# Sixteen-head attention with ALiBi: bias factors on GpSimd, replication in six DMAs

## The reference, cut to what matters

```python
# B = 16, S = 256, C = 128, H = 16 heads of D = 8
x = x + single_head_attention(layernorm(x))       # block 1
x = x + routed_experts(layernorm(x))              # block 2, 8 experts, top 2
h = layernorm(x)                                  # the third norm
qkv = h @ in_proj_weight.T + in_proj_bias
rel = pos[:, None] - pos[None, :]
bias = minimum(rel * slopes[h], 8.0)              # slopes[h] = 2 ** (-0.5 * (h + 1))
scores = q @ k.T * D ** -0.5 + bias
x = x + softmax(scores) @ v @ out_proj_weight.T + out_proj_bias   # block 3
x = x + one_of_8_experts(layernorm(x))            # block 4
```

## Time and profile before

| | us |
|---|---|
| median of 3 runs | 988.57 (988.5 to 989.13) |
| profiled execution, its own time | 988.53 |
| its span, first to last instruction | 986.5 |
| block 3, first to last `score` (L1569) | 477.3 to 784.4 |
| PE busy | 783.2 (79%) |
| DVE busy | 549.3 (56%) |
| ACT busy | 395.9 (40%) |
| POOL busy | 357.9 (36%) |
| DMA queue of SP, share of 16 engines | 27.3% |

### The profile page before, as it was taken

How to read it: one execution, slowest core, us unless ns; L and a number is a source line. 1 busy time by engine, 2 the same in 40 slices (tenths; PEclk the granted TensorE clock), 3 DMA queues, 4 the chain that set the end, 5 groups by cost and what they waited for, 6 DMA issues and landing times.

```text
span 986.5 us, 19021 instructions
## 1 busy us (share of the span) xinstructions
PE 783.2 (79%) x5641; PEld 564.8 (57%) x5641; DVE 549.3 (56%) x2190; ACT 395.9 (40%) x947; POOL 357.9 (36%) x543
## 2 busy tenths in 40 slices
PE   0798479999999999952489999999999982038894
PEld 0676355555666677742246676667666651028883
DVE  4688573233322332333588989898987714026672
ACT  0456121222212322210036666766676661025562
POOL 5000517777850134433222423242322102744552
PEclk9999668999999999986569999999999995559997
DMA  9970001111100132303654444444443014111110
GB/s 250 155 221 0 0 1 36 40 41 41 44 0 14 52 112 78 96 30 90 128 106 95 90 108 93 102 83 106 95 85 67 3 45 155 54 53 55 50 50 14
DMA packets 75114, 72.44 MB, mean 73 GB/s; under 512 B 8125, under 2 KB 65680, under 8 KB 72732
## 3 DMA queue, kind: packets, MB, share of 16 engines
q1 hardware_dynamic: 69436, 60.38, 27.3%
q0 software_dynamic: 5600, 11.12, 3.5%
HBM read 43.71 MB, written 27.33 MB: 72 GB/s over the span
## 4 chain that ended last, share of the span: by engine, by line
PE 52%; DVE 18%; issue 12%; DMA 5%; POOL 5%; ACT 3%; DVEq 2%; SPq 2%; POOLq 0%; ACTq 0%
PE bank L1475 10%; PE bank L1476 9%; DVE rt L1065 6%; PE bank L1498 6%; PE bank L1527 4%; PE bank L1617 3%; PE bank L1569 3%; POOL sorted_rows L766 3%; PE bank L1604 3%; PE bank L1599 2%; DMA arena<-arena 2%; SPq L548 1%; DVEq L1180 1%; PE bank L1435 1%; PE bank L1707 1%
## 5 line engine op out<-in xcount | busy, mean ns | idle before, releaser
L1065 DVE CUSTOM_DVE_ANT_0 rt<-bank,alibi 128x256 f32<-128x256 f32 x512 | 192.9, 419 | 44.4 <-PE bank L1569 37.5
L973 DVE TENSOR_TENSOR arena<-arena,bank 128x512 f32<-128x512 f32 (+1 forms) x128 | 75.0, 587 | 187.8 <-ACT arena L1253 187.8
L1280 ACT ACTIVATE arena<-bank 128x512 f32<-128x512 f32 x256 | 150.6, 598 | 55.4 <-PE bank L1604 49.5
L1253 ACT ACTIVATE arena<-bank 128x512 f32<-128x512 f32 (+1 forms) x128 | 66.1, 517 | 202.9 <-PE bank L1476 202.9
L1569 PE MATMUL bank<-arena 72*128 72x256 bf16 x512 | 104.7, 289 | 26.6 <-DMA arena<-qk_parts 13.4
L1599 PE MATMUL bank<-arena 81*128 81x256 bf16 x512 | 117.0, 274 | 8.3 <-ACT arena L1280 4.7
L1475 PE MATMUL bank<-arena 128*128 128x320 f32 (+2 forms) x256 | 115.7, 534 | 7.5 <-DVE arena L973 7.5
L1476 PE MATMUL bank<-arena 128*128 128x320 f32 (+2 forms) x256 | 111.9, 519 | 0.0
L1604 PE MATMUL bank<-arena,ident_b 128*128 128x256 bf16 (+8 forms) x544 | 80.2, 243 | 0.0
L1569 PEld LDWEIGHTS bank<-arena 72*128 72x128 bf16 x512 | 39.0, 102 | 69.4 <-DVE arena L1065 42.8
L1475 PEld LDWEIGHTS bank<-arena 128*128 128x128 f32 x256 | 42.8, 193 | 53.5 <-DVE arena L973 41.1
(11 more groups left out here) (242 smaller groups left out, 1402.9 us busy)
## 6 DMA issues: line engine op xcount, KB each, us to landing
arena<-qk_parts SPq DMA_DIRECT2D x48, 192.0 KB
arena<-qk_parts SPq DMA_DIRECT2D x144, 64.0 KB
qk_parts<-arena SPq DMA_DIRECT2D x16, 384.0 KB, 2.8
back_rows<-empty_row SPq DMA_DIRECT2D x1, 4096.0 KB, 37.8
arena<-back_rows SPq DMA_DIRECT2D x16, 256.0 KB, 3.8
arena<-in_w SPq DMA_DIRECT2D x2, 2048.0 KB, 10.9
xg_rows<-empty_row SPq DMA_DIRECT2D x1, 2580.0 KB, 38.5
arena<-xg_rows SPq DMA_DIRECT2D x8, 322.5 KB, 4.0
```

The lines of the kernel that those rows point to most:

```text
L973: nc.vector.tensor_tensor(out, sil[:, k, 0:out.shape[1]], bank[4 + k][:, 0:out.shape[1]], ALU.mult).then_inc(hid_done, 1)
L1065: last = nc.vector.tensor_tensor_reduce(biased[n % 2 * QT + u], bank[n % 2][:, SEQ * u:SEQ * u + SEQ], alibi[:, h, P * (1 - u):P * (1 - u) ...
L1253: nc.scalar.activation(sil[:, k, 0:width], bank[2 + k][:, 0:width], ACT.Silu).then_inc(sil_done, 1)
L1280: nc.scalar.activation(prT3[:, n % (2 * HG)].rearrange("p k t -> p (k t)"), bank[2 + n % 2][:], ACT.Exp).then_inc(exp3_done, 1)
```

## The change

The change touches block 3 and its constants.

- **Bias as a factor.** `FULL` goes from 4 to 2. Heads 2 to 8 get no strips on PE. A table `factor` = exp(min(8 - slope * rel, 0)) is built in advance on POOL and ACT, and `apply_factor` (POOL, L782) multiplies the capped columns of the probabilities of heads 2 to 8, after `exponent`, in place. `weigh` waits for `factored`. `prT3` has 12 buffers, not 8.
- **Slots.** `weigh` is cut in halves (`WEIGH_0`, `WEIGH_1`), three slots later than before; `project` in `project_v` and `project_qk`, one slot apart; `copy_qk` in `copy_q` and `copy_k`; `norm5` in two. Most other offsets move by a few slots. POOL goes by the slot table too, where it went batch by batch.
- **Third norm.** `normalise` runs on ACT; `root` on POOL makes scale and shift in four instructions, not one. `values` moves to ACT without its bias; `bv` goes through `w_out` once, ahead of block 3, and is added to `bo`. `v3` has five buffers.
- **Maxima.** `send_max` is issued by ACT, on its own queue, a slot after the copy.
- **Replication.** One DMA of 72 rows for `ks`, with a source that repeats three times; five for `qs`, of 16, 16, 16, 16 and 8 rows, three of them with a source that repeats twice.

```diff
@@
-FULL = 4
+FULL = 2
+PR = 3 * HG
+VRING = 5
...
-COMBINE_0, COMBINE_1, STATS, VARIANCE, NORM, TURN, HT, QKV, QK_COPY, VALUES = -41, -40, -39, -38, -33, -30, -29, -26, -25, -19
...
+COMBINE_0, COMBINE_1, STATS, VARIANCE, ROOT, NORM_0, NORM_1, OUTPUT_BIAS = -42, -41, -38, -37, -36, -34, -33, -29
+TURN, HT, VALUE, QK, Q_COPY, K_COPY, PARTS_QK, VALUES = -32, -31, -27, -26, -25, -24, -23, -21
...
@@
         def replicate(c):
...
             rows = part_dram[c % 2].rearrange("w a (d h) t -> w (a d) h t", d=HD)
-            for a in range(PARTS):
-                r = PARTS * HD * a
-                sp.dma_start(ks[r:r + PARTS * HD, c % RING], rows[1]).then_inc(qk3_in[c % RING], 16)
-                for k in range(PARTS):
-                    sp.dma_start(qs[r + HD * k:r + HD * k + HD, c % RING], rows[0, HD * a:HD * a + HD]).then_inc(qk3_in[c % RING], 16)
+            sp.dma_start(ks[0:KROWS, c % RING], rows[1].unsqueeze(0).to_broadcast([PARTS, PARTS * HD, NH, SEQ])).then_inc(qk3_in[c % RING], 16)
+            for b in range(0, PARTS * PARTS, 2):
+                first, last = b // PARTS, min(b + 1, PARTS * PARTS - 1) // PARTS
+                n = min(2, PARTS * PARTS - b)
+                src = rows[0, HD * first:HD * first + HD * n] if last > first else rows[0, HD * first:HD * first + HD].unsqueeze(0).to_broadcast([n, HD, NH, SEQ])
+                sp.dma_start(qs[HD * b:HD * (b + n), c % RING], src).then_inc(qk3_in[c % RING], 16)
...
@@
+        def apply_factor(n):
+            c, h = divmod(n, NH)
+            pool.wait_ge(exp3_done, n + 1)
+            if n == FULL:
+                pool.wait_ge(factor_set, 1)
+            for k in range(QT):
+                first = capped_from(h, k)
+                if first < SEQ:
+                    pr = prT3[:, n % PR, k, first:SEQ]
+                    last = nc.gpsimd.tensor_tensor(pr, pr, factor[:, h - FULL, first - P * k:SEQ - P * k], ALU.mult)
+            last.then_inc(factored, 1)
...
@@
-        def norm3(c):
...
-                last = nc.vector.tensor_scalar(h3[:, c % 2, u, :], x[:, 2 * c + u, :], mv[:, c % 2, u, 0:1], rstd3[:, c % 2, u:u + 1],
-                                               ALU.subtract, ALU.mult)
...
+        def normalise(c, u):
...
+            last = nc.scalar.activation(h3[:, c % 2, u, :], x[:, QT * c + u, :], ACT.Identity, scale=norm3[:, c % 2, u, 1:2],
+                                        bias=norm3[:, c % 2, u, 0:1])
...
+        def send_max(c):
+            wait_apart(act, (max_rows_done, c + 1))
+            act.dma_start(qs[MROW:KALL, c % RING], max_rows[0:PARTS * NH, c % 2]).then_inc(max_in[c % 2], 16)
...
@@
-                first = bias_from(h, k) if h < CLAMPED else SEQ
-                biases = range(BIAS_PARTS[h]) if first < SEQ else ()
+                biases = range(BIAS_PARTS[h]) if h < FULL else ()
...
+        def weigh(g, u):
...
+            if u == 0:
+                pe.wait_ge(exp3_done, HG * (g + 1))
+                if k * HG < CLAMPED:
+                    pe.wait_ge(factored, factors_to(HG * g + HG - 1))
```

More of the change, by code:

```diff
@@ L82, with capped_from, factors_to @@
 SLOPE_PARTS = [bf16_parts(s) for s in SLOPES]
[L83 to L89, removed]
+BIAS_PARTS = [len([v for v in SLOPE_PARTS[h] if v]) for h in range(FULL)]
+STRIP = [sum(BIAS_PARTS[:h]) for h in range(FULL)]
+FACTORS = CLAMPED - FULL
+def capped_from(h, k):
+    return min((P * k + int(MAX_BIAS / SLOPES[h]) + 1) // 2 * 2, SEQ)
+def factors_to(n):
+    c, h = divmod(n, NH)
+    return FACTORS * c + min(max(h + 1 - FULL, 0), FACTORS)
 def batch_at(slot, offset):
@@ L259, in _build @@
     bn3 = carve([P, 2, QT, 6])
-    mv = carve([P, 2, QT, 3])
-    rstd3 = carve([P, 2, QT])
+    mv = carve([P, 2, QT, 2])
+    norm3 = carve([P, 2, QT, 2])
     h3 = carve([P, 2, QT, D])
@@ L742, in root5 @@
         def root5(e):
-            shift, scale = xw[:, QT * e:QT * e + QT, D + 2], xw[:, QT * e:QT * e + QT, D + 3]
             pool.wait_ge(var5_done, e + 1)
[L747 to L756, removed]
+            root(mv5[:, e % 2], xw[:, QT * e:QT * e + QT, D + 2], xw[:, QT * e:QT * e + QT, D + 3], rstd5_done)
+        def apply_factor(n):
+            c, h = divmod(n, NH)
+            pool.wait_ge(exp3_done, n + 1)
[7 more added lines that the diff above has]
+            last.then_inc(factored, 1)
+        for slot3 in range(FIRST_SLOT, LAST_SLOT):
+            n = head_at(slot3, FACTOR)
+            if n is not None and FULL <= n % NH < CLAMPED:
+                apply_factor(n)
+            if (c := batch_at(slot3, PARTS_QK)) is not None:
                 parts(c)
-            if alive(c + 1, BATCH):
-                root(c + 1)
-            if alive(c, BATCH):
+            if (c := batch_at(slot3, ROOT)) is not None:
+                root3(c)
+            if (c := batch_at(slot3, OUTPUT_BIAS)) is not None:
                 output_bias(c)
-            if alive(c - ROOT_LAG, BATCH):
-                root5(c - ROOT_LAG)
+            if (c := batch_at(slot3, ROOT_5)) is not None:
+                root5(c)
         def send_sorted(i):
@@ L1129, in _ @@
                 norm3_variance(c)
-            if (c := batch_at(slot3, NORM)) is not None:
-                norm3(c)
-            if (c := batch_at(slot3, VALUES)) is not None:
-                values(c)
             if (c := batch_at(slot3, DIVIDE_0)) is not None:
@@ L1292, in turned, with values, copy_q @@
             if c >= 1:
-                act.wait_ge(v3_mm, c)
+                act.wait_ge(qk3_mm, c)
             nc.scalar.activation(hT3, bank[6][:, 0:SEQ], ACT.Copy).then_inc(hT3_done, 1)
-        def copy_qk(c):
+        def values(c):
+            act.wait_ge(v3_mm, c + 1)
+            if c >= VRING:
+                act.wait_ge(pv3_mm, NH // HG * (c - VRING + 1))
+            for u in range(QT):
+                last = nc.scalar.activation(v3[:, c % VRING, u, :, 0:HD],
+                                            bank[6][:, SEQ + D * u:SEQ + D * u + D].rearrange("p (h d) -> p h d", d=HD), ACT.Copy)
+            last.then_inc(v3_done, 1)
+        def copy_q(c):
             act.wait_ge(qk3_mm, c + 1)
```

224 lines of the change are left out of this document (123 added, 101 removed).

## The result

| | before | after |
|---|---|---|
| median, us | 988.57 | 1075.61 (1073.9 to 1088.77, 5 runs) |
| ratio, 95% interval | | 1.0906 [1.0847, 1.0964] |
| mean granted clock of PE | 0.906 | 0.828 in the profiled run, 0.85 in the next ones |
| a batch of block 3, us | 19.4 | 25.8 in the profiled run |

The change makes the kernel 87 us slower by the medians (a ratio of 1.088; the ratio over all runs is 1.0906); 42 were forecast. The profiled run of after is the longest of the five (span 1087.0), so its trace shows the loss some 13 us too large.

A forecast was written before the change was run, and what follows sets the result against it. Replication, confined to two or three DMA engines, was to become block 3's bound, 21.9 us a batch instead of 19.38: 988.5 + 37.8 + 6.5 - 3 + 0.5, together +42, 1030 us; range 953 to 1145, the forecast's own 995 to 1075.

The forecast's parts named there:

- Engine counts: Replication: a DMA uses as many engines as its outermost dimension allows, so repeating sources run on three and two.
- rival 1: Replication: copies spread over up to 16 engines and stay hidden, 958 us in all (950 to 972); chance 0.15.
- The engines' need: Block 3: PE 16.8, DVE 16.5 and ACT 16.8 us a batch, so 17.7 expected instead of 19.38.
- Theory C: Experiments' theory for block 3: edits other than replication and maxima (POOL's factors, ACT's new work, moved slots) cost the time.
- The row: Replication: one row of 8 KB takes 0.35 us on its engine, with 0.315 and 0.73 kept as alternatives.
- The chain's cycle: Replication in block 3: once it is the bound, a batch takes 4.4 + 50 x 0.35 = 21.9 us.
- the fixed part: Replication: 4.4 us a batch that don't scale with the rows, as part's write queues behind the previous batch's rows.
- The first replication: Ahead of block 3's first score: 13.9 us become 2.9 + 50 x 0.35 = 20.4, +6.5 us.
- The sum for the chain alone: Whole kernel, with replication as block 3's bound: +42 us on 988.5, so 1030 us.
- rival 3: Replication: engines reading the same row, or the maxima, hinder one another; over 1075 us, chance 0.29; over 1145, 0.14.
- The turns: send_max on its own queue: its 16 rows per engine alternate with 8 KB rows, landing up to 5.6 us late.
- rival 4: PE's clock in block 3: if it falls in each wait, 16.8 us become up to 20, inside the cycle; no chance given.

The follow-up runs named there:

- e14_twelve_no_max: The changed kernel with the twelve replication DMAs of before and PE not waiting for the maxima (softmax subtracts a constant): 0.9754 of the kernel before.
- e8_four: The changed kernel with replication in four DMAs whose repetition is the inner dimension, rows in another order: 0.9744 of the kernel before, 964 us.
- e13_six_no_max: The changed kernel, six replication DMAs kept, with PE not waiting for the maxima (softmax subtracts a constant): 1.0554 of the kernel before.
- e11_filler: The changed kernel with 36 idle matmuls on PE ahead of each wait for the maxima, in batches 1 to 12: 1.0798 of the kernel before.
- e1_twelve: The changed kernel with the twelve replication DMAs of before, everything else as changed: 1.035 of the kernel before, 1020 us.
- e3_max_on_sp: The changed kernel with the maxima sent from SP's queue again, the six replication DMAs kept: 1.0889 of the kernel before.
- e9_strided: The changed kernel with twelve replication DMAs, each writing every third partition: 0.9769 of the kernel before.

## Why the prediction was right in kind and too small

- **Engine counts.** Right, and with it the fall of rival 1: 3, 2, 16, 2, 2 and 8 small packets.
- **The engines' need.** 17.7 us a batch were forecast for a replication that stays hidden, and 958 us in all (rival 1). `e14_twelve_no_max` has 17.8, `e8_four` 18.0 and 0.9744 x 988.57 = 963 us. Theory C has nothing left: POOL's factors and ACT's new work are hidden.
- **The row.** 0.35 taken, 0.32 measured within a replication. The first rows, with many engines active, are slower (up to 1.3 us), so the 50 rows last 18.4 us (forecast: 17.5).
- **The chain's cycle.** 4.4 + 50 x 0.35 = 21.9 forecast; 22.6 in `e13_six_no_max`. The rows last 18.5 us there, so the fixed part is 4.1, not 4.4.
- **The first replication.** 20.4 forecast. It is issued at 464.09 and the first `score` starts at 483.30, so 19.2.
- **The sum for the chain alone.** 1030 forecast; 1.0554 x 988.57 = 1043. These are 13 of the 45 us that were missing (48 by the ratio): 15 x 0.7 = 10 from the cycle, and 3 that no run isolates. Part of them may belong to `e13_six_no_max` alone: four more start-up DMAs go ahead of its first replication, whose rows start at 473.3, against 469.9 to 471.5 in the four kernels with the maxima that ran on the same chip.
- **The step that failed** is in the sum: it has no term for the maxima. The prediction put them down under rival 3, as another way that it could go, where `send_max` lands up to 5.6 us late "three slots before PE needs it", and left them out of the 1030. The runs showed that they are no alternative to the chain but come on top: the rows that make the chain long stand beside the maxima on the same engines. In ten of the sixteen batches 7.5 to 10.0 us pass from issue to landing, where 1.9 do without a replication, so 4 to 7 us over the three slots' 3.3 us. The turns were sized about right, 3.4 to 5.6 us in those ten. What rival 3 didn't have are the 4.0 to 4.9 us before the first row moves on an engine that is busy with rows; why it takes that long is open. The price is 3.1 points by the medians and 3.5 by the ratios (1.0906 - 1.0554), 31 to 35 us.
- **Which wait ends last.** PE's 17.8 us, 3.7 us a batch of waiting for the maxima and what the half clock adds behind the waits give 25.8, over the chain's 22.6, which fits that PE waits at L1654 and not at L1625. How the remaining 4 us divide between the clock and other waits isn't shown.
- **The clock** (rival 4) was said to stay inside the cycle. Once the engines and not the chain are late, the half clock lengthens what they do; `e11_filler` points that way and doesn't prove it.
- Before, the 0.46 us in the earlier trace rows came 5.1 us after the issue of `send_max` at 618.60. That row already said that the transfer had used up its cover (the slots between its issue and its use); I read it for the price of the issue and not for what stood behind it.

## What to carry to other kernels

A DMA whose source repeats should repeat on the inside: an outermost dimension of 24 or 8 with the repetition behind it used 12 or 8 engines, the same copies with the repetition outermost 3 or 2. When a bulk transfer gets longer, look at the small transfers that share its engines and at how many microseconds each has left to its deadline, and price both; a wait of 0.5 us for one of them means that its cover is gone. Where several engines write at once, leave room between their partitions: here that was worth 4 points.

## What the runs showed of the hardware

- Eight engines that write eight neighbouring partitions moved 98 GB/s (`e1_twelve`); with partitions three apart, 143 (`e8_four`). A row of 8 KB took 0.71 and 0.43 us with as many packets in flight.
- A small DMA on a queue of its own was no faster where its engines were busy (`e3_max_on_sp`: 1.0889, the change: 1.0906). Beside six DMAs its rows alternated with rows of 8 KB, one by one, 0.34 us for a pair; behind twelve (`e1_twelve`) it was late in seven batches, 5.2 to 10.3 us: there its first row started 4.8 to 8.7 us after the issue, and in the batch shown when the rows were through. Why these two differ is open.
- A DMA with a step of three partitions took SP 0.70 us to issue, one without 0.33, so that the 9.2 us of `e9_strided` are nearly all issue time:

```profile
575.38 0.70 SPq L542 DMA_DIRECT2D arena<-qk_parts  x1
```

- After a wait of 5.7 us that ended at 669.90 PE was at half clock until 700, and busy without a gap from 676 on, before its clock rose.
